# Cross-attention of a decoder layer on one core: transposes of a piece and weighting matmuls of the piece two back, interleaved one by one on TensorE

## The reference

```python
qh = _split_heads(jnp.einsum('bnq,qi->bni', x, Wq))         # (8, 2048, 128)
kh = _split_heads(jnp.einsum('bmc,ci->bmi', context, Wk))   # (8, 4096, 128)
vh = _split_heads(jnp.einsum('bmc,ci->bmi', context, Wv))
sim = jnp.einsum('hid,hjd->hij', qh, kh) * SCALE
mean = jnp.mean(sim, axis=-1, keepdims=True)
sim = (sim - mean) * ATTN_MATRIX_SCALE + mean
attn = jax.nn.softmax(sim, axis=-1)
out = jnp.einsum('hij,hjd->hid', attn, vh)
...
return jnp.einsum('bni,iq->bnq', out, Wout) + bout
```

## Time and profile before

| | |
|---|---|
| runs, us | 2820.21, 2821.69, 2823.96 (median 2821.69) |
| profiled execution, us | 2821.53 |
| its span from first to last instruction, us | 2819.7 |
| mean granted TensorE clock | 0.972 of full |
| PE busy | 2608.1 us, 92% |
| PEld busy | 2328.3 us, 83% |
| DVE busy | 1967.0 us, 70% |
| ACT busy | 1594.1 us, 57% |

### The profile page before, as it was taken

One profiled execution on the slowest core, in us unless ns is written; L12 is line 12 of the kernel. 1 busy time (PEld: TensorE's weight loads), 2 busy tenths in 40 slices (PEclk: granted clock), 3 DMA queues, 4 the chain that ended last, 5 costly groups with the idle time before them and its releaser, 6 DMA issues. The chain is left out here.

```text
span 2819.7 us, 47515 instructions
## 1 busy us (share of the span) xinstructions
PE 2608.1 (92%) x17664; PEld 2328.3 (83%) x17664; DVE 1967.0 (70%) x3680; ACT 1594.1 (57%) x3005; POOL 132.6 (5%) x153
## 2 busy tenths in 40 slices
PE   6477777799999999999999999999999999999976
PEld 4466666599989988998899889988998899889975
DVE  6366667577767777776777677767776777677776
ACT  4366662366656664665565655655565566556644
POOL 0450002100000000000000000000000000000003
PEclk9799999799999999999999999999999999999987
DMA  5563321500030002001100120011001100110000
GB/s 177 166 166 80 81 53 51 192 23 15 16 113 16 23 28 93 20 18 55 66 24 15 61 68 16 15 60 68 16 15 60 68 16 23 53 63 23 8 12 30
DMA packets 94881, 152.85 MB, mean 54 GB/s; under 512 B 48400, under 2 KB 62096, under 8 KB 93680
## 3 DMA queue, kind: packets, MB, share of 16 engines
q1 hardware_dynamic: 90176, 137.48, 15.3%
q0 software_dynamic: 3200, 12.59, 1.3%
q10 hardware_dynamic: 1328, 0.39, 0.1%
HBM read 123.02 MB, written 23.20 MB: 52 GB/s over the span
## 5 line engine op out<-in xcount | busy, mean ns | idle before, releaser
L1292 ACT CAST pt_hi<-xt_ps 128x512 fp32r<-128x512 f32 x1024 | 592.5, 585 | 574.9 <-PE xt_ps L1262 558.9
L1358 DVE TENSOR_TENSOR pt_lo<-xt_ps,pt_hi 128x512 fp32r<-128x512 f32 x1024 | 704.7, 688 | 265.3 <-ACT pt_hi L1292 262.1
L1347 DVE TENSOR_SCALAR_CACHE_REDUCE xprobs<-xs_ps 128x1024 f32<-128x1024 f32 x512 | 626.7, 1224 | 175.3 <-PE xs_ps L1211 170.5
L1273 PE MATMUL xo_ps<-pt_hi,v_hi 128*128 128x256 f32 x2048 | 649.5, 317 | 1.3 <-DVE pt_lo L1358 1.3
L1298 ACT ACTIVATE xprobs<-xprobs,xneg_max 128x1024 f32<-128x1024 f32 x512 | 591.5, 1155 | 26.7 <-DVE xneg_max L1353 26.7
L1262 PE MATMUL xt_ps<-ident,xprobs 128*128 128x128 f32 x4096 | 604.2, 272 | 0.0
L1273 PE MATMUL xo_ps<-pt_lo,v_hi 128*128 128x256 f32 x2048 | 577.6, 282 | 0.0
L1273 PE MATMUL xo_ps<-pt_hi,v_lo 128*128 128x256 f32 x2048 | 576.1, 281 | 0.0
L1262 PEld LDWEIGHTS xt_ps<-ident,xprobs 128*128 128x128 f32 x4096 | 485.0, 140 | 60.7 <-issue 6.9
L1273 PEld LDWEIGHTS xo_ps<-pt_hi,v_hi 128*128 128x128 f32 x2048 | 388.8, 190 | 4.0 <-DVE pt_lo L1358 1.3
L1273 PEld LDWEIGHTS xo_ps<-pt_lo,v_hi 128*128 128x128 f32 x2048 | 389.4, 190 | 1.9
(11 more groups left out here) (203 smaller groups left out, 2842.4 us busy)
## 6 DMA issues: line engine op xcount, KB each, us to landing
blocks<-ctx_split SPq DMA_DIRECT2D x68, 768.0 KB, 5.7
xq<-x_split SPq DMA_DIRECT2D x64, 512.0 KB, 3.2
q_st<-rel_split SPq DMA_DIRECT2D x64, 128.0 KB, 2.5
q_st<-q_split SPq DMA_DIRECT2D x192, 32.0 KB, 2.0
k_st<-k_split SPq DMA_DIRECT2D x192, 32.0 KB, 1.9
ctx_split<-ctx_out POOLq DMA_DIRECT2D x8, 768.0 KB, 4.3
v_st<-v_split SPq DMA_DIRECT2D x64, 64.0 KB, 2.3
x_split<-xq_out SPq DMA_DIRECT2D x8, 512.0 KB, 4.8
```

What stands on the lines that cost most here:

```text
L1273: last = pe.matmul(o_ps[:, 0:GQ], v[:, vs], pt[:, c % 3, GQ * j:GQ * (j + 1)], start=c == 0 and j == 0 and m == 0, stop=c == PIECES - 1 an ...
L1292: act.copy(pt_hi[:, c % 3, :], t_ps[:, c % 3, :]).then_inc(t_rounded, 1)
L1347: dve.tensor_scalar(probs[:, par if kind == "A" else 1 - par, t, CHUNK * i:CHUNK * (i + 1)], s_ps[:, buf, :], LOGIT, None, ALU.mult, ALU.m ...
L1358: dve.tensor_tensor(pt_lo[:, c % 3, :], t_ps[:, c % 3, :], pt_hi[:, c % 3, :].bitcast(F32), ALU.subtract).then_inc(t_ready, 1)
```

## The change: one for one

Within an item T(c) with c of 2 or more, PE now issues the six weighting matmuls of piece c-2 between the transposes: transpose, one weighting matmul, transpose, two, transpose, one, transpose, two. The item W(c-2) then does nothing on PE for these pieces; W(14) and W(15), which have no transposes beside them, are issued as before. T(0) and T(1) are as before. Nothing is added or taken away; ACT's and DVE's instructions, their order, their waits and all DMAs are the same.

```diff
+            def weights(c, items, s):
+                if c == 0 and items is not STEP_1 and items is not LAST_1:
+                    pe.wait_ge(o_ready, s - 1)
+                pe.wait_ge(t_ready, s * PIECES + (c + 1 - PIECES))
+                for j in range(2):
+                    vs = slice(P * (2 * c + j), P * (2 * c + j + 1))
+                    for m, (v, pt) in enumerate(((v_hi, pt_hi), (v_hi, pt_lo), (v_lo, pt_hi))):
+                        last = pe.matmul(o_ps[:, 0:GQ], v[:, vs], pt[:, c % 3, GQ * j:GQ * (j + 1)],
+                                         start=c == 0 and j == 0 and m == 0,
+                                         stop=c == PIECES - 1 and j == 1 and m == 2)
+                        if j == 1 and m == 2:
+                            last.then_inc(o_done if c == PIECES - 1 else weighed, 1)
+                        yield
...
-                        for j in range(2):
-                            for t in range(2):
-                                last = pe.transpose(t_ps[:, c % 3, GQ * j + P * t:GQ * j + P * (t + 1)],
-                                                    probs[:, 1 - par, t, P * (2 * c + j):P * (2 * c + j + 1)], ident[:])
-                        last.then_inc(turned, 1)
-                    elif kind == "W":
...
+                        weighing = weights(c - 2, items, s) if c >= 2 else iter(())
+                        for n_turn, (j, t) in enumerate([(j, t) for j in range(2) for t in range(2)]):
+                            last = pe.transpose(t_ps[:, c % 3, GQ * j + P * t:GQ * j + P * (t + 1)],
+                                                probs[:, 1 - par, t, P * (2 * c + j):P * (2 * c + j + 1)], ident[:])
+                            if n_turn == 3:
+                                last.then_inc(turned, 1)
+                            for _ in range(1 + n_turn % 2):
+                                next(weighing, None)
+                    elif kind == "W" and item[1] >= PIECES - 2:
+                        for _ in weights(item[1], items, s):
+                            pass
```

## The result

The changed kernel takes 2834.99 us (median of 4 runs, 2833.24 to 2839.53), the kernel before 2820.95 in the same comparison (4 runs, 2817.42 to 2823.96). The ratio is 1.0053 with a 95% interval of 1.0035 to 1.0070: slower, by 14 us. 2833.4 was predicted.

What follows compares the result with a forecast made beforehand. PE's pace was taken to bound the kernel. 8.1 us for changes of kind plus 3.6 us of waits made 11.7 us on 2821.53, 2833.2; the median 0.16 higher gave 2833.4 us, range 2820 to 2847.

Steps and rivals of the forecast that it cites:

- What bounds the kernel: PE bounds it, busy for all 30.89 us of a regular step; ACT and DVE delays cost nothing within their reserve.
- Only one load runs ahead, so interleaving gains nothing: On PE, each matmul starts no sooner than one weight load, about 0.109 us, after the one before; no first-order gain.
- the faster rival: Loads on PE run further ahead once short and long streams alternate: 56 us less, 2769 us with the waits; chance 0.04.
- The pair of changes of kind: Three more transpose-to-weighting-and-back pairs in 14 pieces of 64 steps, 3 ns each: 8.1 us, possibly -11 to +24.
- The later release and the earlier wait: Fourth transpose 0.48 us later, first weighting matmul 0.33 sooner; free in regular steps, 3.6 us of waits elsewhere.
- Reserve 0.81 less: Slack before a piece's weighting shrinks by 0.81 us; regular steps keep 0.49 at piece 9, 0.32 at piece 0.
- A head's first step: PE waits 0.2 us for W(9), where pieces 9, 10, 11 follow each other; once a head, 1.6 us in all.
- The step before the last: ACT already runs behind there and its work starts 0.48 us later, so PE ends about 0.5 us later.
- The last: In the last step, waits at W(0), some 0.7 us from piece 7 to 15, and late W(14), W(15): 1.5 us.
- Where to see it: Signs: piece of ten 1.16 us, regular step some 31.0, new PE idle for `pt_lo` only in ten steps, 3 to 4 us.

Runs made afterwards that it cites:

- swapped blocks: Against the kernel before, the six weighting matmuls of piece c-2 stand as one block ahead of the four transposes of piece c: 2842.22 us, ratio 1.0078.
- two and three: Against the changed kernel, each piece issues two transposes, three weighting matmuls, two transposes, three weighting matmuls: 2830.21 us, ratio 1.0034 to the kernel before.

## Why the prediction was right, point by point

**What bounds the kernel.** Right, and now shown: with ACT and DVE thinned to a third the regular step is unchanged to 1 ns in either order.

**Only one load runs ahead, so interleaving gains nothing.** Right. The 0.23 to 0.24 from transpose to transpose over one weighting matmul, and a step that grew, leave no room for the faster rival. Loads do run ahead, but by one and no more: no load of the 40 regular steps starts before the matmul in front of its own.

**The pair of changes of kind, 3 ns, 8.1 us.** The term is under-sized: measured 0.173 / 42 = 4.1 ns, 11.1 us, within the -4 to +9 that I gave. But its form, so many pairs at a fixed price, fell. One added pair per piece costs 7.6 ns, three cost 12.4 together, and swapped blocks cost 0.147 a step with no pair added inside a piece. That the term still came near its size is in part luck: it was read from starts rounded to 10 ns, which left -11 to +24 us open, and the same 3 ns a pair would have given 0.04 us a step for two and three, where 0.107 was measured, and nothing for the swapped blocks, where it was 0.147.

**The later release and the earlier wait.** Right place by place. Reserve 0.81 less: piece 9 of a regular step had 1.30 and now has 0.52, piece 0 had 0.65 and has 0.31 to 0.32, no regular step waits. (Not all other pieces had more than these two, as the prediction says: piece 15 had 1.08, and keeps 0.62.) A head's first step: 0.2 predicted, 0.17 beyond the pace. The step before the last: 0.5 and 0.53. The last: 1.5 and 1.7. Sum 3.6 us, and 3.6 measured. The run with interleaving only in those ten steps came within 0.1 us in its trace.

**Where to see it.** The regular step at "some 31.0" was 31.06, a piece followed at once by the next 1.16 to 1.17. Wrong was that 3 to 4 us of new idle time for `pt_lo` would stand on PE: its list went from 1.3 to 1.9, since a wait shorter than a matmul's record is hidden by it.

**What stays open.** Why a stream's pace shifts by 1 or 2 ns with what stands around it. It isn't ACT's and DVE's traffic, the operands' values or the granted clock (1.00 in every regular step shown); 0.13 of 0.17 us goes when the transposes become ordinary matmuls. For the swapped blocks, where scores got slower, no run tells more.

## What to carry to other kernels

First ask what sets the distance behind each kind of matmul, its stream or the next load, and whether loads run ahead by more than one: here they didn't, and shuffling short and long matmuls moved no load into cover. What did pay was fewer matmuls with more columns for the same weights, by 0.3%. A transpose that feeds two other engines belongs as early, and a wait as late, as the order allows: what an interleaving takes from that reserve can be read off the trace before, subtraction by subtraction.

## What the runs showed of the hardware that was not expected

- The length of a step depends on the order of its matmuls at the level of 0.3 to 0.6%, with the same matmuls, full clock and no waits: 30.887, 30.994, 31.033 and 31.060 us for four orders. It repeats over the 40 regular steps of each trace to 15 ns.
- ACT and DVE, busy with PSUM and SBUF for 61% and 73% of a step, slow PE by nothing measurable: the steps are 30.887 and 31.060 us with that work and with a third of it.
- A step with transposes is 0.16 us shorter than one with 64 ordinary matmuls of 128 columns in their place.
- The load of a transpose's weights starts late behind a weighting matmul: 17 ns after that matmul's start before the change and 23 after it (mean over the regular steps), where the load of another weighting matmul starts 2 to 3 ns after. Before, this was caught up (119.3 ns from start to start, as between two weighting matmuls); after, the distance is 121.6. Whether the late load causes it is not shown.
